# Adding the experts' rows straight into the output, with a bound that leaves empty places out

## What is computed

```python
logits = xm @ router_w.T + router_b
probs = jax.nn.softmax(logits, axis=-1)
topw, topi = jax.lax.top_k(probs, K)                  # K = 2 of E = 8 experts
topw = topw / jnp.sum(topw, axis=-1, keepdims=True)
combine = jnp.zeros((T, E), xm.dtype).at[jnp.arange(T)[:, None], topi].add(topw)
out = jnp.zeros_like(xm)
for e in range(E):
    h = jax.nn.gelu(xm @ w1[e] + b1[e], approximate=False)
    y = h @ w2[e] + b2[e]
    out = out + combine[:, e:e + 1] * y
x = x + out.reshape(B, S, D)
```

## Time and profile before

| | |
|---|---|
| time, median of 3 runs | 2126.27 us (2124.63 to 2131.35) |
| time of the profiled execution | 2131.68 us |
| its span, first to last instruction | 2130.0 us |
| PE / DVE / ACT / POOL busy | 75% / 62% / 46% / 19% of the span |
| expert part | from about 1740 us to the end |

### The profile page before, as it was taken

One profiled execution on the slowest core, in us unless ns is written; L12 is line 12 of the kernel. 1 busy time (PEld: TensorE's weight loads), 2 busy tenths in 40 slices (PEclk: granted clock), 3 DMA queues, 4 the chain that ended last, 5 costly groups with the idle time before them and its releaser, 6 DMA issues.

```text
span 2130.0 us, 35436 instructions
## 1 busy us (share of the span) xinstructions
PE 1599.1 (75%) x12060; PEld 1166.6 (55%) x12060; DVE 1313.0 (62%) x4361; ACT 977.8 (46%) x2773; POOL 400.1 (19%) x494
## 2 busy tenths in 40 slices
PE   0166765966777568888888768888888859999996
PEld 0032224855555445555555546666666637777775
DVE  7898885877777777778878735555555531221221
ACT  1367998833333445554554423333333314434342
POOL 7302331000000100000000001222122223333332
PEclk9985555578777679999999968777777769999998
DMA  3000001089900000000000000000000027777775
GB/s 71 14 1 1 1 1 20 3 162 191 178 5 0 1 1 1 0 0 0 0 0 0 1 25 12 24 23 19 15 22 22 23 82 185 173 178 184 175 177 133
DMA packets 136262, 112.99 MB, mean 53 GB/s; under 512 B 29417, under 2 KB 128457, under 8 KB 136137
## 3 DMA queue, kind: packets, MB, share of 16 engines
q1 hardware_dynamic: 119320, 91.70, 18.4%
q0 software_dynamic: 16864, 20.33, 5.0%
HBM read 69.19 MB, written 45.94 MB: 54 GB/s over the span
## 4 chain that ended last, share of the span: by engine, by line
PE 54%; DVE 26%; ACT 13%; issue 4%; POOL 1%; DVEq 0%; DMA 0%; another core or an unknown queue 0%; ACTq 0%; POOLq 0%; SPq 0%
ACT bank L716 8%; PE bank L2323 8%; PE bank L1007 7%; PE bank L2308 5%; PE bank L2312 4%; PE bank L1988 3%; PE bank L966 3%; PE bank L1219 2%; PE bank L1000 2%; PE bank L1666 2%; PE bank L2001 2%; DVE WK L1840 1%; DVE WK L1582 1%; DVE R L1582 1%; DVE R L1840 1%
## 5 line engine op out<-in xcount | busy, mean ns | idle before, releaser
L1047 POOL TENSOR_TENSOR WK<-WK,mhalf 128x2 f32<-128x2 f32 (+1 forms) x96 | 77.9, 812 | 906.0 <-DVE WK L1506 326.9
L2360 ACT ACTIVATE R<-bank,R 128x256 f32<-128x256 f32 x234 | 98.3, 471 | 217.0 <-PE bank L2312 217.0
L2212 DVE SCALAR_TENSOR_TENSOR WK<-bank,R,WK 128x192 f32<-128x192 f32 x78 | 28.9, 413 | 264.1 <-PE bank L2323 264.1
L1007 PE MATMUL bank<-WK,R 96*128 96x256 f32 x576 | 177.5, 465 | 15.9 <-ACT WK L973 11.0
L716 ACT ACTIVATE bank<-bank,nbias,sc 128x128 f32<-128x128 f32 x384 | 168.9, 954 | 20.5 <-POOL nbias L528 20.5
L2241 POOL DMA_INDIRECT moe_sum<-WK x78 | 121.5, 1558 | 257.6 <-DVE WK L2212 190.5
L2323 PE MATMUL bank<-R 128*128 128x192 f32 x936 | 169.1, 331 | 0.0
L716 ACT ACTIVATION_READ_ACCUMULATOR bank<-bank,nbias,sc 128x1 f32 x384 | 162.5, 729 | 0.0
L2323 PEld LDWEIGHTS bank<-R 128*128 128x128 f32 x936 | 150.1, 190 | 13.3 <-issue 13.3
L1007 PEld LDWEIGHTS bank<-WK,R 96*128 96x128 f32 x576 | 130.9, 237 | 43.5 <-ACT WK L973 15.6
L966 PE MATMUL bank<-ident,WK 128*96 128x128 f32 x320 | 67.2, 348 | 85.3 <-DVE WK L1030 68.7
(11 more groups left out here) (493 smaller groups left out, 3936.3 us busy)
## 6 DMA issues: line engine op xcount, KB each, us to landing
moe_rows_in<-zeros SPq DMA_DIRECT2D x1, 25026.0 KB, 139.4
R<-in_L_ffn_w SPq DMA_DIRECT2D x39, 576.0 KB
R<-in_L_ffn_w SPq DMA_DIRECT2D x39, 384.0 KB
R<-moe_rows_in SPq DMA_DIRECT2D x39, 194.0 KB, 4.5
R<-in_L_ffn_w SPq DMA_DIRECT2D x78, 96.0 KB
R<-in_L_ffn_b SPq DMA_DIRECT2D x39, 96.0 KB
moe_sum<-resid POOLq DMA_DIRECT2D x16, 192.0 KB
moe_sum<-WK POOLq DMA_INDIRECT x78, 5.8
```

What stands on the lines that cost most here:

```text
L1007: mm = nc.tensor.matmul(out, w[0:C, c, m], a.xT[0:C, c, :], start=(c == 0), stop=(c == 1))
L1047: nc.gpsimd.tensor_tensor(a.rs[:, 0:n], a.ve[:, 0:n], mhalf[:, 0:n], ALU.pow).then_inc(f.root, 1)
L2360: ins = nc.scalar.activation(x_hid[q], bank[(0, 2, 0)[p] + n][:, 0:NR], ACT.Gelu, bias=xb_1[h][:, q:q + 1])
```

## The change

The adds now go to the output tensor itself. `acc` is the name of the output's rows, which has 4096 of them, with none to spare. So `send` copies the residual rows there as well. Each add carries a bound of 4095: a row whose index is greater is to be left out without an error. The copy at the end and its wait are gone.

```diff
-        acc = nc.dram_tensor("moe_sum", (T * P + NR, D), F32).ap()
+        acc = out.rearrange("t p d -> (t p) d")
...
                     pool.indirect_dma_start(out=acc, out_offset=bass.IndirectOffsetOnAxis(
                         ap=x_id[k % B3][:, t:t + 1].bitcast(U32), axis=0), in_=x_y[k % B3][:, t, :], in_offset=None,
-                        compute_op=ALU.add).then_inc(x_add, 16)
+                        compute_op=ALU.add, bounds_check=T * P - 1, oob_is_err=False).then_inc(x_add, 16)
...
             sp.wait_ge(x_add, 32 * NX)
-            flat = lambda x: x.rearrange("r d -> (r d)").rearrange("(p n) -> p n", p=P)
-            sp.dma_start(flat(out.rearrange("t p d -> (t p) d")), flat(acc[0:T * P, :])).then_inc(x_end_st, 16)
-            sp.wait_ge(x_end_st, 16)
```

## The result

The changed kernel takes 2117.64 us in the median of 13 runs (2115.56 to 2124.14), the kernel before 2127.76 us in 13 runs (2124.63 to 2132.7). The ratio is 0.9956 with a 95% interval of 0.9946 to 0.9967, that is 9.4 us less (7.0 to 11.5); the two medians themselves lie 10.1 us apart. The forecast was 2113.9 us (2108 to 2121), 12.4 us less.

The account below looks back on a forecast made before the run. PE was taken to pace the expert part, with an uncovered end of POOL's last adds and the output copy. The terms −11.6 + 0.1 + 0 − 0.9 = −12.4 us took 2126.27 to 2113.9 us, range 2108 to 2121.

Parts of the forecast that it names:

- a new wait of some us behind the last landing: At the program's end: listed among the profile signs that would show the forecast wrong; size given only as some us.
- The copy and its wait: Program's end, SP's copy into the output: its whole 11.6 us from issue to landing leave the path, −11.6 us.
- the final waits of 0.5 us: Program's end: 0.5 us between the copy's landing and the span's end, expected to stay behind the last add.
- The empty places: Last group's two adds, holding only empty places: with no data to move, the last landing shortens by 0.9 us.
- The estimate of 0.23 us: Last add's data: the skill page values an add's 98,304 bytes at 0.23 us, making the sum 2114.6 us.
- the lower bound of −2.1 us: Program's end: most that skipping empty rows could save, if issuing both last adds also got shorter.
- The bound: Index check on each POOL add: extra cost between about −0.59 and +0.59 us, taken as 0.
- d: Each POOL add instruction: extra issue time from its index check, between about −0.59 and +0.59 us, taken as 0.
- the rival on the other side: Expert part: POOL becomes the bound if each add costs 0.33 us more; up to 2133.8 us, chance 0.10.
- POOL's own chain: Expert part, per group: 1.85 + 6.4 + 0.4 = 8.65 us against a step of 9.37, median slack 0.7 us.
- Register moves: Ahead of each add, 29 ns: hidden in POOL's slack for 38 groups, last group's two on the path, +0.1 us.
- The residual rows into the output: Ahead of the expert part: the same 16 transfers at the same places, written to the output instead, costed at nothing.

## Why the prediction was right, and where it was off

The direction, the range and the mechanism held. The size held less well: −12.4 us lies outside the measured interval (7.0 to 11.5 us less). The stated range, 2108 to 2121 us, is 13 us wide, mostly for the spread of the runs, and so had room for a term that is wrong by 4.2 us; its lower end of 2109, ahead of the stretching, does not follow from its own terms, which give 2113.9 − 1.2 − 1.6 = 2111.1. One of the prediction's own signs of being wrong did appear: a new wait of some us behind the last landing, 4.4 us. And that the two profiled spans differ by 14.3 us, where 12 were expected, is luck, since the tail gives only 8.0 of them. By the prediction's own terms:

- **The copy and its wait, −11.6 us.** This is the step that failed: "the final waits of 0.5 us stay behind the last add instead". What stays is 4.7 us (2111.0 to 2115.7), because POOL's drain of 4.2 us came out from under the copy. From the last landing to the end it was 12.1 us and is now 4.7, a saving of 7.4 us; with the copy alone removed 7.5 us were measured. The mechanism was right and this term too large by 4.2. I named the work that hides each edit, but did not ask what the removed piece itself had been hiding. It could be seen in the trace of before, by asking for the line of the last wait.
- **The empty places, −0.9 us.** Measured −0.65 us with the bound alone (3.38 to 2.73 us to land); in the changed kernel POOL goes on 2.7 us after the last add's start (2108.31 to 2111.0), which agrees. The estimate of 0.23 us from the Trainium skill, "DMA: Bandwidth & Descriptors", section "Anatomy of one DMA — SWDGE (gpsimd) path", was further off. The issue still takes 1.55 us and each row keeps its packet, so the lower bound of −2.1 us was not in play.
- **The bound, 0.** Right: 1.55 us, d under 0.01. Thus POOL stayed out of the way, and the rival on the other side needed 0.33 by the prediction's working. That it would bind there is argued and not shown, and one trace speaks against it: when the drain of 5.0 us made POOL late, a whole step took 6.20 us, less than the 8.65 us that the prediction counts for POOL's own chain. A later add can thus land sooner, as the prediction allowed.
- **Register moves, +0.1 us.** The last group's first add starts 0.84 us after DVE's end, before 0.77: +0.07.
- **The residual rows into the output, 0.** Nothing to be told: run again, the changed kernel gains 7.4 us (5.1 to 9.7), and its tail alone gives 8.0.

The terms measured give −7.4 − 0.65 + 0.07 = −8.0 us, the difference between the two tails, and inside both intervals. The 1.4 us from there to the 9.4 of the result are within its noise.

## What to carry to other kernels

When the last piece of a chain is removed, look at what ran beneath it up to the end of the program, sequencer rows included, and not only at the engines' busy time. Ask for the line of the final waits: an engine that issues its transfers in software may have a long drain there, as POOL has here. If the drain is bare, an earlier one in a gap where that engine idles takes its work away; its own 3.6 to 5.0 us have to fit in there. Here one added drain took 3.9 us off the 10.1 that the changed kernel needed behind DVE's end.

## What the runs showed of the hardware

- POOL's DRAIN took 4.195 us at the end of a program in which POOL had issued 190 transfers, though all its adds had landed. It grew by 0.0817 us with each add since the last drain, up to 40. Beyond that it is not simply longer with more: 3.969 us with 78 adds since the last drain, and with 150, 170, 186, 188 and 190 transfers since the program's start 3.582, 5.012, 3.868, 4.032 and 4.195 us. What the work is, and what takes some of it away in between, was not settled.
- Placed right behind the scatters and residual copies, without a wait for them, a drain had a row of 13.2 us. Five of these transfers were still being issued inside it, and 7.3 us lie behind the last; how much of them was waiting for transfers was not separated.
- An indirect add whose 128 rows all lie beyond the bound costs POOL the same 1.55 us and the same number of packets, of 8 bytes instead of 768, and lands after 2.7 us instead of 3.4.
